# First routing's norms, turns and logits moved into the first attention's program

## The chip, the cores and the metric

The kernel runs on one core of a Trainium2 chip. The metric is device time in microseconds of one execution. In the rows PE is TensorE (PEld its weight loads), DVE is VectorE, ACT is ScalarE, POOL is GpSimd and SP is SyncE, which issues the transfers.

## The reference, cut to what matters

```python
x = x + attention0(layernorm(x), ctx, ctx, mask, Wq, Wk, Wv, Wo)       # 4 x 512 tokens of 256, 16 heads of 64
x = x + ffn0(layernorm(x), gate_w, gamma, beta, fc1s, b1s, fc2s, b2s)
x = x + attention1(layernorm(x), ...)
x = x + ffn1(layernorm(x), ...)

def ffn0(x, ...):                                   # 2048 tokens, 8 experts
    scores = (tanh(xf @ gate_w.T) + 1) * 0.5
    vals, idx = top_k(scores.T, 256)                # each expert picks its 256 tokens
    y = layernorm(xf[idx]) * gamma + beta           # then two layers, times vals, added to xf at idx
```

## The kernel before

Each layer is a program of its own (an `nc.Block`): all engines meet at its end. The first two matter here. All batches' x stay in SBUF as `T.x`, 16 tiles of 128 tokens by 256.

**`phase_attention0`** goes through 256 units in order. A unit `u` is 128 queries of one head against 512 keys; eight units (`UNITS`) make a head pair `g = u // 8`, `j = u % 8` counts within it, and eight pairs make a batch. Each engine has its instructions in an order written out by hand, and runs its loop over `u` with a lag: PE multiplies scores of u (`score`, L460), transposes the exponentials of u-3 (`turn`, L468) and multiplies them by the values of u-5 (`attend`). DVE takes the masked maximum of u (`maximum`, L677) and the low half of the transposed block of u-3 (L651), ACT the exponential of u (L576) and the high half of u-3 (L569). Most products are three fp16 products of high and low parts (`three_products`, L70 to L72). PE's score of u waits for the maximum of u-2 (two banks `sc`).

Between them stands side work, given by `side_work(g, j)` and done by PE at the end of unit (g, j): the k and q projections of the next pair at j = 0 and 1, a v projection for the next batch at j = 4, the output projection of the batch before at j = 5 (`w`, added to `T.x` by DVE), and the transposes of the next batch's normalized rows at j = 5 of pairs 5 and 6 (`z`). These groups use two banks `pj` in turn: a group waits until the one two places before it has been read (`open_group`). A `direct` group is read by ACT (high part) and DVE (low part) one unit later; the others go through ACT, POOL and SP. The statistics for the z groups are done on DVE in single steps (`late_statistics`): bn_stats, bn_aggr, and an inverse square root by an integer guess and three Newton steps, two steps in every three units from unit 6 of a batch on. After the last unit comes a tail: the last output projections (`late_products`), added to `T.x` by DVE (L778).

**`phase_route0`** then computes the layer norm of all four batches again (statistics L1067, L1070, Sqrt on ACT L944, norms on DVE L1085 and ACT L953), transposes it (L1009), copies it (L948), multiplies it in fp32 by the gate (`route`, L1016), takes Tanh (L974), and finds each expert's 256th largest score by a search of nine rounds: DVE compares all scores with seven candidates (`compare`, L1114), PE counts (L1031), DVE narrows (L1123 to L1127). After it come prefix sums on PE (L1034 to L1037), slots and lists of tokens (up to L1177). Beside the search ACT writes the expert rows `y` (L977) and the sum `T.x * (1 + rstd)` (L984), which SP stores (`acc`, `y`). SP's first loads, for this layer and the experts, stand at this program's start.

## Time and profile before

| what | us |
|---|---|
| three runs | 1173.72, 1176.66, 1181.28 (median 1176.66) |
| the profiled execution | 1175.02 |
| its span | 1173.1 |

By the page of the profile PE is busy for 91% of the span, DVE for 65%, ACT for 58%, POOL for 45%. The page cuts the span into 40 slices of 29.3 us. The first seventeen are the attention program; the granted clock, in tenths, is 9 in all of them and 8, 5 and 6 in slices 18 to 20, around the routing. A timeline row gives start and length in us; "x4" with one length is a run of instructions that follow each other, and the brackets name the engine's idle time just before and what ended it.

### The profile page before, as it was taken

Reading aid. Unit: us, or ns where it says so; the run is one execution under the profiler, and the core shown is the slowest. Engines: PE = TensorE matmul, PEld = TensorE weight load, DVE = VectorE, ACT = ScalarE, POOL = GpSimd, SP = SyncE. Lnnn points to the kernel's source line nnn. Section 1 sums busy time; section 2 is a strip of 40 time slices with the busy share of each in tenths; the row PEclk is TensorE's granted clock in tenths of the full one; section 3 lists DMA queues with packets and bytes.
Section 4 is the critical chain, followed back from the end, with each engine's and each line's share of the span. In section 5 each row is a group of like instructions: output and inputs, shape, how many; then the busy total and the mean of one; then the engine's idle time right before and its main releaser. Section 6 shows DMA issues by size and latency. Waiting matters only on the chain. (4 is left out here: it accounts for less than half of the span.)

```text
span 1173.1 us, 28682 instructions
## 1 busy us (share of the span) xinstructions
PE 1065.8 (91%) x10231; PEld 785.1 (67%) x10232; DVE 759.5 (65%) x2183; ACT 676.7 (58%) x1282; POOL 529.1 (45%) x599
## 2 busy tenths in 40 slices
PE   6999999999999999966699999698998866999996
PEld 3666777767777777666388886344454445888885
DVE  5888888888878877956611116668777774455553
ACT  6878876777768776837232216357667643343331
POOL 4677545465356433310147740566667523233312
PEclk9999999999999999985699999899999977999998
DMA  7633432333333422243546636624444241111110
GB/s 255 167 74 86 88 74 73 92 82 73 76 68 94 93 69 69 62 154 122 172 139 192 187 64 188 187 65 123 139 122 143 61 134 37 29 27 31 27 14 10
DMA packets 120027, 116.16 MB, mean 99 GB/s; under 512 B 43488, under 2 KB 100064, under 8 KB 119776
## 3 DMA queue, kind: packets, MB, share of 16 engines
q1 hardware_dynamic: 112608, 105.27, 31.9%
q0 software_dynamic: 7296, 9.25, 4.7%
q8 instruction: 77, 1.26, 0.4%
q14 instruction: 46, 0.38, 0.1%
HBM read 59.89 MB, written 21.82 MB: 70 GB/s over the span
## 5 line engine op out<-in xcount | busy, mean ns | idle before, releaser
L576 ACT ACTIVATE e<-masked,neg_max 128x512 f32<-128x512 f32 x256 | 184.4, 720 | 47.0 <-DVE neg_max L677 44.2
L651 DVE TENSOR_TENSOR e_t_lo<-et,e_t_hi 128x512 f16<-128x512 f32 x256 | 176.4, 689 | 46.1 <-ACT e_t_hi L569 43.9
L677 DVE CUSTOM_DVE_ANT_0 masked<-sc,mask_bias 128x512 f32<-128x512 f32 x256 | 175.3, 685 | 28.3 <-issue 24.5
L569 ACT ACTIVATE e_t_hi<-et 128x512 f16<-128x512 f32 x256 | 151.2, 591 | 68.3 <-PE et L468 67.0
L468 PEld LDWEIGHTS et<-ident,e 128*128 128x128 f32 x1024 | 124.5, 140 | 57.4 <-issue 8.9
L468 PE MATMUL et<-ident,e 128*128 128x128 f32 x1024 | 154.4, 273 | 1.2 <-ACT e L576 0.8
L2140 ACT ACTIVATE d_e<-d_st 128x384 f32<-128x384 f32 (+1 forms) x192 | 94.0, 526 | 49.4 <-PE d_st L2283 44.6
L70 PE MATMUL ob<-v_hi,e_t_hi 128*128 128x65 f16 x1024 | 119.0, 193 | 1.2 <-issue 1.2
L71 PE MATMUL ob<-v_lo,e_t_hi 128*128 128x65 f16 x1024 | 119.2, 193 | 0.0
L72 PE MATMUL ob<-v_hi,e_t_lo 128*128 128x65 f16 x1024 | 118.4, 193 | 0.0
L70 PE MATMUL h_hb<-h_xt_hi,experts_hi 128*128 128x256 f16 x352 | 96.8, 275 | 3.8 <-DVE h_xt_lo L2514 3.8
L460 PE MATMUL sc<-kk,qq 128*128 128x512 f16 x254 | 96.1, 378 | 2.9 <-DVE neg_max L677 1.9
L71 PE MATMUL h_hb<-h_xt_lo,experts_hi 128*128 128x256 f16 x352 | 96.8, 275 | 0.0
L72 PE MATMUL h_hb<-h_xt_hi,experts_lo 128*128 128x256 f16 x352 | 96.8, 275 | 0.0
L70 PEld LDWEIGHTS ob<-v_hi,e_t_hi 128*128 128x128 f16 x1024 | 95.7, 97 | 1.4 <-issue 1.4
L71 PEld LDWEIGHTS ob<-v_lo,e_t_hi 128*128 128x128 f16 x1024 | 94.5, 97 | 2.9
L461 PE MATMUL sc<-kk,qq 128*128 128x512 f16 x254 | 96.1, 378 | 0.0
L72 PEld LDWEIGHTS ob<-v_hi,e_t_lo 128*128 128x128 f16 x1024 | 94.7, 97 | 0.0
L2501 ACT ACTIVATE h_silu<-h_hb 128x256 f32<-128x256 f32 x88 | 33.7, 383 | 105.4 <-PE h_hb L72 105.4
L2288 PE MATMUL d_wk<-qk 128*128 128x384 f16 (+1 forms) x256 | 72.5, 311 | 12.5 <-PEq L1428 7.2
L2179 DVE TENSOR_REDUCE d_mx<-d_wk 128x1 f32<-128x384 f32 x128 | 66.3, 552 | 25.1 <-PE d_wk L2293 21.2
L2098 POOL TENSOR_SCALAR_AFFINE_SELECT d_e<-d_e 128x384 f32<-128x384 f32 x128 | 62.9, 521 | 43.0 <-ACT d_e L2140 42.9
(466 smaller groups left out, 2758.7 us busy)
## 6 DMA issues: line engine op xcount, KB each, us to landing
kk<-nat_k SPq DMA_DIRECT2D x64, 256.0 KB, 3.5
raw<-in_fc SPq DMA_DIRECT2D x16, 1024.0 KB, 7.5
qq<-nat_q SPq DMA_DIRECT2D x64, 128.0 KB, 2.4
qk<-scratch_stack SPq DMA_DIRECT2D x64, 128.0 KB
scratch_stack<-kq_hi SPq DMA_DIRECT2D x16, 256.0 KB, 3.0
scratch_stack<-kq_lo SPq DMA_DIRECT2D x16, 256.0 KB, 3.1
d_expert_raw<-in_gate_w SPq DMA_DIRECT2D x8, 512.0 KB, 3.8
d_expert_raw<-in_up_w SPq DMA_DIRECT2D x8, 512.0 KB, 3.9
```

Source lines behind the costliest of these rows:

```text
L70: pe.matmul(out, stat[0], mov[0], start=first, stop=False)
L71: pe.matmul(out, stat[0], mov[1], start=False, stop=False)
L72: return pe.matmul(out, stat[1], mov[0], start=False, stop=last)
L460: pe.matmul(sc[j % 2][:], stat, kk[g % 2][:, a, 0, :], start=True, stop=False)
L461: pe.matmul(sc[j % 2][:], stat, kk[g % 2][:, a, 1, :], start=False, stop=True).then_inc(scores, 1)
L468: mm = pe.transpose(et[u % 2][:, kt, :], e[u % NBUF][:, kt * P:(kt + 1) * P], T.ident[:])
L569: nc.scalar.activation(e_t[u % NBUF].hi[:], et[u % 2][:], ACT.Copy).then_inc(turned_hi, 1)
L576: nc.scalar.activation(e[u % NBUF][:], masked[u % NBUF][:], ACT.Exp, bias=neg_max[:, g % 2, j:j + 1], scale=-1.0).then_inc(exp_ok, 1)
L651: nc.vector.tensor_tensor(e_t[u % NBUF].lo[:], et[u % 2][:], e_t[u % NBUF].hi[:], ALU.subtract).then_inc(turned_lo, 1)
L677: nc.vector.tensor_tensor_reduce(masked[u % NBUF][:], sc[j % 2][:], mask_bias[g // PAIRS % 2][:, j % QT, :], -SCALE0, 3e38, ALU.add, ALU.m ...
L2140: nc.scalar.activation(part(e[n % EBUF][:, i // 3, :, :], i % 3), src, ACT.Exp, scale=SCALE1).then_inc(exp_ok, 1)
L2288: mm = pe.matmul(out[:, cols:cols + m * P], stat[n % QBUF][:, a, tile * P:(tile + 1) * P], mov[n % QBUF][:, a, start * P:(start + m) * P], ...
```

## The change

The first part of `phase_route0` goes into `phase_attention0`. Batches 0 to 2 become a new kind of side work, `r`: batch b's statistics are single steps on DVE once all its `w` groups are added, one step a unit from unit 40 of batches 1 and 2, two a unit from unit 40 of batch 3 (`late_steps`; 22 steps a batch, with one more variance than z). Their norms are ACT's, two units ahead of the group, and PE turns them at j = 7 of the first two pairs of the batch after next; for batch 2, at (30, 7) and (31, 3). The turned rows go to `T.z_t` as high and low fp16 parts. In the tail PE multiplies the logits of these 12 tiles as three fp16 products of 8 columns by the split gate; DVE puts the last batch's statistics between its last adds, the rest of the chain follows (Sqrt on ACT, reciprocal, norms on both, turns, parts, logits), and Tanh is the program's last step. `phase_route0` starts with the score. There ACT's `y` and `x` passes come first, with w_hi after the second batch; DVE's split of w1 moves behind the search and that of wo1 behind the first keys; POOL makes the first offsets first.

```diff
+LAST_ROUTE = [(PAIRS0 - 2, 7), (PAIRS0 - 1, 3)]
+LATE_AT, LATE_STEPS = 6, 2 * QT + 13
+ROUTE_AT, ROUTE_STEPS = 40, 2 * QT + 14
...
+    if j == 7 and b >= 2 and p < 2:
+        return "r", (b - 2, p)
+    if (g, j) in LAST_ROUTE:
+        return "r", (B - 2, LAST_ROUTE.index((g, j)))
     return None
+def late_steps(u):
+
+    b, at = u // (PAIRS * UNITS), u % (PAIRS * UNITS)
+    step, route = at - LATE_AT, at - ROUTE_AT
+    if b + 1 < B and step >= 0 and step % 3 < 2 and step // 3 * 2 + step % 3 < LATE_STEPS:
+        return [("z", b + 1, step // 3 * 2 + step % 3)]
+    if b >= 1 and route >= 0:
+        steps = (route,) if b + 1 < B else (2 * route, 2 * route + 1)
+        return [("r", b - 1, n) for n in steps if n < ROUTE_STEPS]
+    return []
...
+                sp.dma_start(gate_raw[:], dram["gate0"].rearrange("(c p) e -> p c e", p=P)).then_inc(gate_in, 16)
...
+                def turn_route(what):
+                    b, i = what[1]
...
+                    pe.wait_ge(r_act, 4 * b + 2 * (i + 1))
+                    for t in range(2):
+                        for c in range(DT):
+                            mm = pe.transpose(out[:, c * 2 * P + t * P:c * 2 * P + (t + 1) * P], late_z[b % 2][i][:, t, c * P:(c + 1) * P], T.ident[:])
+                    mm.then_inc(pj_full, 1)
...
+                def route(t):
+                    for c in range(DT):
+                        mm = three_products(pe, logit[:, t, :], (T.z_t.hi[:, c, t * P:(t + 1) * P], T.z_t.lo[:, c, t * P:(t + 1) * P]),
+                                            (gate_w.hi[:, c, :], gate_w.lo[:, c, :]), c == 0, c == DT - 1)
+                    return mm
...
+                        pe.wait_ge(direct_lo, len(DIRECT0))
...
                 pe.wait_ge(last_lo, 1)
                 for qt in range(QT):
                     late_products(qt, [CT - 1]).then_inc(late_full, 1)
+                pe.wait_ge(turned_lo, units)
+                pe.wait_ge(gate_lo, 1)
+                for t in range(NT - QT):
+                    route(t)
+                for i in range(2):
+                    if i == 0:
+                        pe.wait_ge(z_dve, 4)
+                    else:
+                        pe.wait_ge(r_act, 4 * (B - 1) + 2)
+                    for t in range(2):
+                        for c in range(DT):
+                            mm = pe.transpose(route_banks[i][:, c * 2 + t, :], early_z[2 * i + t][:, c * P:(c + 1) * P], T.ident[:])
+                    mm.then_inc(z_turned, 1)
+                for i in range(2):
+                    pe.wait_ge(z_lo, 2 + i + 1)
+                    for t in range(2):
+                        mm = route(NT - QT + 2 * i + t)
+                mm.then_inc(logits, 1)
...
-                    ahead = side_work(u // UNITS, u % UNITS + 2) if u < units and u % UNITS == 3 else None
+                    if u == GATE_AT:
+                        act.wait_ge(gate_in, 16)
+                        nc.scalar.activation(gate_w.hi[:], gate_raw[:], ACT.Copy).then_inc(gate_hi, 1)
+                    ahead = side_work((u + 2) // UNITS, (u + 2) % UNITS) if u + 2 < units else None
+                    if ahead is not None and ahead[0] == "r":
+                        b, i = ahead[1]
+                        act.wait_ge(late_ok, LATE0["r", b, ROUTE_STEPS - 1] + 1)
+                        act.wait_ge(pj_full, GROUP0["w", (b, QT - 1)] + 1)
+                        for t in range(2):
+                            route_norm(late_z[b % 2][i][:, t, :], b, 2 * i + t)
...
+                act.wait_ge(exp_ok, units)
+                nc.scalar.activation(warm, T.ident[:, 0:1], ACT.Sqrt)
                 act.wait_ge(last_turned, 1)
                 nc.scalar.activation(last_part.hi[:, CT - 1, :], last_bank[:], ACT.Copy).then_inc(last_hi, 1)
+                root(2, sd2)
+                act.wait_ge(shift_ok, 2)
+                for t in range(2, QT):
+                    route_norm(early_z[t], B - 1, t)
+                for i in range(2):
+                    act.wait_ge(z_turned, 2 + i + 1)
+                    cols = slice((B - 1) * S + i * 2 * P, (B - 1) * S + (i + 1) * 2 * P)
+                    nc.scalar.activation(T.z_t.hi[:, :, cols], route_banks[i].rearrange("p (c t) n -> p c (t n)", c=DT), ACT.Copy).then_inc(z_hi, 1)
+                nc.scalar.activation(warm, T.ident[:, 0:1], ACT.Tanh)
+                act.wait_ge(logits, 1)
+                nc.scalar.activation(T.route_tanh[:], logit, ACT.Tanh)
...
+                    done = LATE0[kind, b, n]
+                            dve.wait_ge(added, ADD0["w", (b, n)] + 1)
+                        y, roots, half, power = T.route_rstd[:, b, :, :].rearrange("p r t -> p (r t)"), sd2, halves2, square2
...
+                    elif kind == "r" and n == 2 * QT + 1:
+                        op = nc.vector.tensor_scalar(sd2[:, QT:2 * QT], mv[:, :, 1], 1.0 + EPS, EPS * EPS, ALU.mult, ALU.add)
...
-                        b, step = u // (PAIRS * UNITS) + 1, u % (PAIRS * UNITS) - LATE_AT
-                        if b < B and step >= 0 and step % 3 < 2 and step // 3 * 2 + step % 3 < LATE_STEPS:
-                            late_statistics(b, step // 3 * 2 + step % 3)
+                        if u == GATE_AT + 1:
+                            dve.wait_ge(gate_hi, 1)
+                            nc.vector.tensor_tensor(gate_w.lo[:], gate_raw[:], gate_w.hi[:], ALU.subtract).then_inc(gate_lo, 1)
+                        for step in late_steps(u):
+                            late_statistics(*step)
...
+                def last_statistics(qt):
+                    dve.wait_ge(added, len(ADD0) + qt + 1)
+                    nc.vector.bn_stats(stats[:, qt, :], T.x[:, (B - 1) * QT + qt, :]).then_inc(stat_ok, 1)
...
+                dve.wait_ge(late_ok, len(LATE0))
                 for qt in range(QT):
                     dve.wait_ge(late_full, qt + 1)
                     xt = T.x[:, (B - 1) * QT + qt, :]
                     nc.vector.tensor_tensor(xt, late[qt][:, 0:D], xt, ALU.add).then_inc(added, 1)
-
-
-EXPERTS0 = 8
+                    if qt >= 1:
+                        last_statistics(qt - 1)
+                last_statistics(QT - 1)
+                dve.wait_ge(stat_ok, 3 * QT)
+                for t in range(QT):
+                    nc.vector.bn_aggr(mv[:, t, :], stats[:, t, :]).then_inc(stat_ok, 1)
+                dve.wait_ge(stat_ok, 4 * QT)
+                nc.vector.tensor_scalar(sd, mv[:, :, 1], EPS, None, ALU.add).then_inc(stat_ok, 1)
+                nc.vector.tensor_scalar(sd2[:, QT:2 * QT], mv[:, :, 1], 1.0 + EPS, EPS * EPS, ALU.mult, ALU.add).then_inc(stat_ok, 1)
+                dve.wait_ge(stat_ok, 4 * QT + 2)
+                dve.sem_inc(var_ok, 1)
+                dve.wait_ge(sd_ok, 2)
+                nc.vector.reciprocal(T.route_rstd[:, B - 1, :, :].rearrange("p r t -> p (r t)"), sd2).then_inc(rstd_ok, 1)
+                dve.wait_ge(rstd_ok, 2)
+                route_shift(B - 1).then_inc(shift_ok, 1)
+                dve.wait_ge(exp_ok, units)
+                for t in range(2):
+                    nc.vector.tensor_scalar(early_z[t], T.x[:, (B - 1) * QT + t, :], mv[:, t, 0:1], T.route_rstd[:, B - 1, 0, t:t + 1], ALU.subtract, ALU.mult).then_inc(z_dve, 1)
+                for i in range(2):
+                    dve.wait_ge(z_hi, 2 + i + 1)
+                    cols = slice((B - 1) * S + i * 2 * P, (B - 1) * S + (i + 1) * 2 * P)
+                    nc.vector.tensor_tensor(T.z_t.lo[:, :, cols], route_banks[i].rearrange("p (c t) n -> p c (t n)", c=DT), T.z_t.hi[:, :, cols], ALU.subtract).then_inc(z_lo, 1)
...
-                sp.dma_start(gate[:], dram["gate0"].rearrange("(c p) e -> p c e", p=P)).then_inc(gate_in, 16)
...
+                def offset(r):
+                    pool.tensor_scalar(offsets[:, r, :], offs[:], float(CANDS + 1) ** -(r + 1), None, ALU.mult).then_inc(consts, 1)
+
                 pool.iota(offs[:], pattern=[[1, CANDS]], base=1, channel_multiplier=0, allow_small_or_imprecise_dtypes=True).then_inc(consts, 1)
-                pool.memset(zeros[:], 0.0)
+                pool.wait_ge(consts, 1)
+                offset(0)
+                pool.memset(ones[:], 1.0).then_inc(consts, 1)
+                for r in range(1, ROUNDS):
+                    offset(r)
+                pool.memset(zeros[:], 0.0).then_inc(consts, 1)
                 pool.memset(picks[:, NT, :], 0.0).then_inc(consts, 1)
...
-                nc.scalar.activation(warm[:, 0:1], T.ident[:, 0:1], ACT.Sqrt)
...
-                root(0)
...
-                for b in range(B):
-                    copy(2 * b)
-                    if b + 2 < B:
-                        root(b + 2)
-                    copy(2 * b + 1)
-                    if b + 2 < B:
-                        norm(b + 2)
-                    if b == 1:
-                        act.wait_ge(w_in, 16 * 3)
-                        nc.scalar.activation(T.w1.hi[:], raw[:, 0:2, :, :], ACT.Copy).then_inc(w_hi, 1)
-                        nc.scalar.activation(T.wo1.hi[:], raw[:, 2, :, :], ACT.Copy).then_inc(w_hi, 1)
-                    if b == B - 2:
-                        nc.scalar.activation(warm[:, 1:2], T.ident[:, 0:1], ACT.Tanh)
-                act.wait_ge(logits, 1)
-                nc.scalar.activation(score, logit, ACT.Tanh).then_inc(tanh_ok, 1)
...
                 for b in range(B):
                     for t in range(b * QT, (b + 1) * QT):
                         nc.scalar.activation(y[:, t, 0:D], T.x[:, t, :], ACT.Identity, bias=shift[:, b, 1, t % QT:t % QT + 1],
                                              scale=rstd[:, b, 1, t % QT:t % QT + 1]).then_inc(y_done, 1)
-                    act.wait_ge(more_ok, b + 1)
-                    act.wait_ge(xf_dve, 2 * (b + 1))
-                    act.wait_ge(xf_act, 2 * (b + 1))
+                    act.wait_ge(more_ok, 1)
                     act.wait_ge(y_done, (b + 1) * QT)
                     for t in range(b * QT, (b + 1) * QT):
                         op = nc.scalar.activation(T.x[:, t, :], T.x[:, t, :], ACT.Identity, bias=shift[:, b, 0, t % QT:t % QT + 1],
                                                   scale=more[:, b, t % QT:t % QT + 1])
                     op.then_inc(sum_done, 1)
+                    if b == 1:
+                        act.wait_ge(w_in, 16 * 3)
+                        nc.scalar.activation(T.w1.hi[:], raw[:, 0:2, :, :], ACT.Copy).then_inc(w_hi, 1)
+                        nc.scalar.activation(T.wo1.hi[:], raw[:, 2, :, :], ACT.Copy).then_inc(w_hi, 1)
...
-                def route(g):
-                    pe.wait_ge(copied, g + 1)
-                    for t in range(2 * g, 2 * g + 2):
-                        for c in range(DT):
-                            mm = pe.matmul(logit[:, t, :], xf_t[:, c, t * P:(t + 1) * P], gate[:, c, :], start=(c == 0), stop=(c == DT - 1))
-                    return mm
-
-                pe.wait_ge(gate_in, 16)
-                turn(0)
-                for g in range(NT // 2):
-                    if g + 1 < NT // 2:
-                        turn(g + 1)
-                    mm = route(g)
-                mm.then_inc(logits, 1)
-                pe.wait_ge(consts, TRI)
+                pe.wait_ge(consts, ONES)
...
+                pe.wait_ge(consts, TRI)
...
-                for b in range(B):
-                    nc.vector.tensor_scalar(more[:, b, :], rstd[:, b, 0, :], 1.0, None, ALU.add).then_inc(more_ok, 1)
-                dve.wait_ge(w_hi, 2)
-                nc.vector.tensor_tensor(T.w1.lo[:], raw[:, 0:2, :, :], T.w1.hi[:], ALU.subtract).then_inc(T.w1_split, 1)
-                nc.vector.tensor_tensor(T.wo1.lo[:], raw[:, 2, :, :], T.wo1.hi[:], ALU.subtract)
                 ahead(nc.vector.tensor_reduce(own[:], T.ident[:].rearrange("p (e d) -> p e d", d=DIGIT), AX.X, ALU.max))
-                ahead(nc.vector.tensor_reduce(eighth[:], T.ident[:].rearrange("p (j a) -> p a j", a=8), AX.X, ALU.max))
-                ahead(nc.vector.tensor_reduce(column[:], T.ident[:].rearrange("p (j a) -> p j a", a=8), AX.X, ALU.max))
-                dve.wait_ge(consts, OFFSETS)
+                nc.vector.tensor_scalar(score, T.route_tanh[:], 1.0, 0.5, ALU.add, ALU.mult).then_inc(score_ok, 1)
+                dve.wait_ge(consts, OFFSET0)
                 for h in range(2):
                     ahead(nc.vector.tensor_copy(cand[h][:], offsets[:, 0, :].unsqueeze(2).to_broadcast([P, CANDS, HE])))
                     ahead(nc.vector.memset(found[h][0][:, 0, :], 0.0))
                 dve.wait_ge(v, steps[0])
-                dve.wait_ge(tanh_ok, 1)
-                nc.vector.tensor_scalar(score, score, 1.0, 0.5, ALU.add, ALU.mult).then_inc(score_ok, 1)
                 dve.wait_ge(score_ok, 1)

...
                 compare(0)
                 compare(1)
+                nc.vector.tensor_scalar(more[:], rstd[:, :, 0, :], 1.0, None, ALU.add).then_inc(more_ok, 1)
+                    if r + 1 < ROUNDS:
+                        dve.wait_ge(consts, ONES + r + 1)
...
+                dve.wait_ge(w_hi, 2)
+                nc.vector.tensor_tensor(T.w1.lo[:], raw[:, 0:2, :, :], T.w1.hi[:], ALU.subtract).then_inc(T.w1_split, 1)
+                ahead(nc.vector.tensor_reduce(eighth[:], T.ident[:].rearrange("p (j a) -> p a j", a=8), AX.X, ALU.max))
+                ahead(nc.vector.tensor_reduce(column[:], T.ident[:].rearrange("p (j a) -> p j a", a=8), AX.X, ALU.max))
...
+                dve.wait_ge(consts, IDS)
...
+                nc.vector.tensor_tensor(T.wo1.lo[:], raw[:, 2, :, :], T.wo1.hi[:], ALU.subtract)
...
```

## Rows read from the trace of the kernel before

**Rows 1.** Stages: length, busy us (instructions) of each engine, clock, DMA share, GB/s
```profile
258.00:380.00 122.00, 121.98 (x1411) 90.05 (x1408) 99.42 (x316) 91.98 (x159) 63.65 (x69) 1.00 0.35 79
...
512.50:540.90 28.40, 20.24 (x96) 19.78 (x96) 15.09 (x71) 14.29 (x29) 3.28 (x16) 0.58 0.67 224
```
**Rows 2.** Timeline of DVE, from the last adds to the routing's end
```profile
510.96 0.75 DVE L778 TENSOR_TENSOR x<-sc,x 128x256 f32<-128x256 f32 x2 [0.60 <-PE sc L72]
...
512.70 1.40 DVE L1067 BATCH_NORM_STATS2 r_stats<-x 128x6 f32<-128x256 f32 x4 [0.32 <-PEq L233]
...
516.81 0.20 DVE L1080 RECIPROCAL r_rstd<-r_sd 128x8 f32<-128x8 f32 x1
...
530.28 1.22 DVE L1098 TENSOR_TENSOR w_lo<-r_raw,w_hi 128x1024 f16<-128x1024 f32 x1 [3.46 <-ACT wo_hi L970]
...
540.87 1.16 DVE L1114 TENSOR_TENSOR r_flags<-r_y,r_cand 128x448 f16<-128x448 f32 x2
...
566.10 0.17 DVE L1139 TENSOR_SCALAR r_need<-r_prefix_bank 128x8 f32<-128x8 f32 x1 [2.66 <-PE r_prefix_bank L1037]
...
576.90 0.17 DVE L1177 CAST slot_token<-r_slot_bank 128x16 int32<-128x16 f32 x1 [0.29 <-PE r_slot_bank L1048]
```
**Rows 3.** Timeline of ACT, the attention's tail and the routing's front
```profile
509.05 0.60 ACT L639 ACTIVATE o_t_hi<-pj 128x512 f16<-128x512 f32 x1 [5.81 <-PE pj L547]
512.67 1.28 ACT L940 ACT_TABLE_LOAD   x1 [3.03 <-PEq L233]
...
514.83 0.21 ACT L944 ACTIVATE r_sd<-r_sd 128x8 f32<-128x8 f32 x1 [0.66 <-DVE r_sd L1074]
517.25 1.09 ACT L953 ACTIVATE r_xf<-x,r_shift,r_rstd 128x256 f32<-128x256 f32 x2 [2.22 <-DVE r_shift L1083]
...
540.23 0.28 ACT L974 ACTIVATE r_y<-r_score_bank 128x128 f32<-128x128 f32 x1 [2.62 <-PE r_score_bank L1016]
```
**Rows 4.** Timeline of PE: transposes in the tail and in the front, search counts
```profile
508.35 0.65 PE L547 MATMUL pj<-ident,o 128*128 128x128 f32 x4 [0.73 <-DVE o L662]
...
523.62 1.09 PE L1009 MATMUL r_tb<-ident,r_xf 128*128 128x128 f32 x4
...
547.31 0.61 PE L1031 MATMUL r_count_bank<-r_flags,r_ones 128*128 128x28 f16 x16 [0.62 <-DVE r_flags L1114]
```
**Rows 5.** Stages again: head pairs 29 and 31, columns as in rows 1
```profile
459.78:473.05 13.27, 13.08 (x159) 9.21 (x157) 11.49 (x38) 10.66 (x20) 5.32 (x6) 1.00 0.30 70
...
486.16:497.53 11.37, 10.40 (x145) 7.70 (x144) 11.10 (x37) 9.58 (x17) 1.77 (x2) 1.00 0.12 24
```
**Rows 6.** DVE's groups, 30 to 380 us: short z steps; busy us, mean ns
```profile
L717 DVE TENSOR_TENSOR late_words<-n_rstd 128x4 f32<-128x4 f32 x9 | 5.2, 583 | 0.0
...
L721 DVE SCALAR_TENSOR_TENSOR n_rstd<-late_words,n_rstd 128x4 f32<-128x4 f32 x9 | 3.7, 416 | 0.0
...
L719 DVE SCALAR_TENSOR_TENSOR late_words<-late_words 128x4 f32<-128x4 f32 x9 | 2.6, 288 | 0.0
L711 DVE TENSOR_SCALAR late_words<-late_words 128x4 int32<-128x4 int32 x3 | 2.4, 807 | 0.0
```
**Rows 7.** One of these steps in the view of their tile: ns least/median/most
```profile
L719 DVE SCALAR_TENSOR_TENSOR late_words<-late_words x9: 145/152/948, 68.0 to 331.6; 128x4 f32<-128x4 f32 x9
```
**Rows 8.** Timelines of POOL and of DVE about 195 us
```profile
195.18 1.16 POOL L337 TENSOR_TENSOR nat_q<-raw,nat_q 128x512 f16<-128x512 f32 x1
...
195.55 0.80 DVE L717 TENSOR_TENSOR late_words<-n_rstd 128x4 f32<-128x4 f32 x1
```
**Rows 9.** Waits of PE (30 to 130 us), of DVE (138 to 499): total, times, longest
```profile
PE pj L70 <- DVE v_lo L732: 1.7, 2, 1.2
...
DVE z_t_lo L732 <- ACT z_t_hi L592: 2.5, 4, 0.7
```
**Rows 10.** Transfers from 512.5 to 578 us, and one stage among them
```profile
DMA packets 9031, 10.69 MB, mean 163 GB/s; under 512 B 1216, under 2 KB 8384, under 8 KB 8896
...
521.00:524.00 3.00, 2.11 (x10) 2.11 (x11) 2.79 (x14) 2.13 (x6) 0.00 (x0) 0.50 0.98 379
```

## What I expect, and why

> **What bounds the kernel now.** I read the table of stages first. In the attention program PE is busy for all of 122 us between 258 and 380, at clock 1.00, while DVE is busy for 99.4 and ACT for 92.0; the 120 us before and after look the same. So PE sets its pace. In the front of the routing (512.5 to 540.9) PE is busy for 20 of 28 us at clock 0.58, and no engine is the bound there [rows 1]. What is, the timelines show: a chain. The last adds end at 512.38, the statistics of all four batches start on DVE at 512.70, each batch goes through Sqrt, reciprocal and norms, PE transposes it and multiplies it in fp32 by the gate, ACT copies it between the two, and Tanh runs at 540.23; the first compare of the search starts at 540.87 [rows 2 to 4]. Last I asked what room the attention program has for the work that moves into it: a table by head pair [rows 5], the like steps that are there already [rows 6 to 8], and their waits [rows 9].
>
> **What the change takes away.** From the first of the four last adds (510.96) to the first compare (540.87) are 29.9 us [rows 2]. In the new order this stretch holds, on the path:
> - four adds and four statistics in turn on DVE, eight at 0.34 (two adds take 0.75, four statistics 1.40), the last one 0.41: 2.8;
> - aggregates and two tensor_scalars, from the statistics' end at 514.10 to ACT's Sqrt at 514.83: 0.7; Sqrt 0.25; reciprocal to ACT's first norm (516.81 to 517.25): 0.45 [rows 2, 3];
> - two norms on ACT 1.1 [rows 3]; four transposes of the second half, 0.65 at full clock (just after the attention) or 1.09 (in the front) [rows 4]. The logits of three batches now keep PE at work until shortly before them, so I take 0.7;
> - ACT's copy to the high part 0.6 [rows 3]; then DVE's low part (some 0.7, twice the 0.34 of an add, for twice its width) and 12 small products (at most 0.46, as 16 of the search's take 0.61 [rows 4]) beside the Tanh table load and its warm-up (1.28, as at 512.67, and 0.2, like a Sqrt). The table is the later: 1.5; Tanh 0.3 [rows 3];
> - the change of program 0.32 (DVE's idle time before 512.70); one reduction, the score and the first candidates, which DVE does in passes of 0.2 to 0.3: 0.8 [rows 2].
>
> Together 9.5, and 0.9 for hops between engines that I can't see: 10.4, bounds 9.9 to 11.4. **Gain 19.5 us (18.5 to 20.0).**
>
> Costed at nothing: the 72 small products for 12 tiles (72 x 0.038 = 2.7 us) on PE, which has nothing to do while DVE works out the last batch; uncovered they cost 2.7. The Sqrt table load (1.28) stands in ACT's 5.81 idle before 509.05 [rows 3]. The split of w1 (1.22) and two small reductions move to where DVE idles for 2.66 before 566.10 [rows 2]. The split of wo1, half as large, waits for nothing and would cost 0.6 uncovered. ACT's 32 row passes (16 x 1.09 us [rows 3]) start a little before the search as they did, and end before it. The gate's 8 KB and their split are two short passes in batch 0. SP's loads start some 8 us later, with the new routing program near 521 (the attention's growth left out), and what needs them is due 19 us earlier: 10.7 MB pass between 512.5 and 578, a busy stretch moves 379 GB/s [rows 10], so some 30 us from 522, over by 553, against the routing's new end near 557 (576.90 less 19.5).
>
> **What the change adds to the attention program**, where PE is the bound. Units count eight to a head pair, pairs 0 to 31.
> - *Six turns.* Four transposes take PE 0.65 [rows 4], some 0.5 of it alone since the next product overlaps the last; four of the turns lie where PE is bound: 2.0. A turn sits in unit 7, and the next pair's q product, two groups on, writes its bank, so PE waits for ACT's high and DVE's low part. The v groups of batch 0 sit in the same place and cost PE 1.7 us over four [rows 9]: 1.7 for four. ACT's two norms in a row delay its copies in pair 24: 0.3. Sum 4.0 (2.0, the transposes alone, to 6.0, every q product waiting 1.0).
> - *66 statistics steps on DVE*, 22 a batch. A statistic takes DVE 0.34, an aggregate 0.1, a short step about 0.1 with nothing in its way. But the like steps of the z batches run longer beside POOL: the one at 195.55 takes 0.80 and ends with POOL's subtraction, at 196.34 [rows 8]. The 27 Newton steps took 11.5 us, and at 0.152, the median of nine of them [rows 7], would have taken 4.1: 0.27 lost on each; the integer shift took 0.81 each time [rows 6]. I take 0.2 lost on a short step, as POOL is busy for only 5.3 of 13.3 us in pair 29 [rows 5].
>   - Batches 1 and 2, one step a unit from unit 40 of the batch: some 6 us a batch over three pairs, with DVE idle for 2.8 us a pair on average (22.6 over 122 us [rows 1]). PE needs a mask only two units later, so most of it fits: 0.3 a pair, 2.0 together (0.5 to 4.0).
>   - Batch 3, two steps a unit, in pairs 29 and 30. DVE's 1.8 idle us in pair 29 [rows 5] lie in units 0 and 1, where PE does the k and q products; in units 2 to 7 its instructions follow each other. What falls into units 0 and 1 (the four statistics, and in pair 30 four Newton steps) fits. The rest of pair 29 is 0.6 for four aggregates, 0.3, 0.95 with the integer shift, and 1.1 for four Newton steps: 2.8 after a little lead; of pair 30, 0.4, and 0.5 as ACT's norms come in between. Pair 31 has no projections, and DVE is busy for 11.10 of 11.37 us [rows 5]. Each of its two turns makes DVE wait for ACT's high part (0.7, the longest such wait [rows 9]) and then takes 0.6; the two norms (1.1) hold up ACT's copy of the turned block: 2.6 + 1.0. Sum 2.8 + 0.9 + 3.6 = 7.3 (5 to 10).
>
> A rule of the Trainium skill speaks against this change: SBUF — State Buffer, section Who interferes with whom, says that VectorE and GpSimd share one pair of ports under an exclusive lock, so that a VectorE instruction with two SBUF inputs, or in a two-port mode, blocks until the GpSimd instruction is through. The trace agrees: the short step ends with POOL's instruction [rows 8]. If each of 42 short steps met the start of a 1.16 us subtraction, they would add 49 us, not my 8.
>
> Sum of the additions 4.0 + 2.0 + 7.3 = **13.3 us** (7.5 to 20).
>
> **Result.** -19.5 + 13.3 = -6.2. The profiled execution took 1175.0 (span 1173.1 and 1.9 around it), so **1169 us**; the median of the runs shown is 1.7 above that execution, and they spread from 1173.7 to 1181.3. Corners: 1175.0 - 20.0 + 7.5 = 1162.5 and 1175.0 - 18.5 + 20.0 = 1176.5.
>
> **The rivals.**
> - *The side work is swallowed (faster).* DVE is idle for 1.8, 1.8 (pair 30 is like pair 29) and 0.3 us in the last three pairs, ACT for 2.6, 2.6 and 1.8 [rows 5], and the z steps left PE busy throughout [rows 1]. If only the turns' transposes and 2.5 us in pair 31 are seen, the growth is 4.5: 1175.0 - 19.5 + 4.5 = 1160. Against it: DVE's idle time is not where the two-a-unit steps lie.
> - *VectorE's short steps stall throughout (slower).* One mechanism: short steps that meet POOL's subtractions make DVE late, PE late behind it, and the next ones meet POOL again. At 1.0 us for each of 42 steps instead of 0.3 the growth is 13.3 + 29 = 42: 1175.0 - 19.5 + 42 = 1198. It makes the kernel 1% slower from 0.6 us of stall a step on, twice the 0.27 of [rows 6].
> - *The routing waits for its transfers.* With the front shorter, loads, sums and rows share 36 us. At the 224 GB/s of the old front as a whole [rows 1] the 10.7 MB need 48 us, end at 570, and 13 us of the gain go: 1182. Against it: the busy stretch moves 379 [rows 10].
>
> **How the numbers follow.** Some 1% (12 us) is what a measurement of this kernel can tell from no change. Forecast 0.63 (its own range 1162 to 1178, with the spread of runs), swallowed 0.23, stalls 0.09, transfers 0.05. Faster by over 1%: 0.23; within: 0.63 + 0.05 = 0.68; slower: 0.09. The range takes in the swallowed case and the forecast's upper corner with the spread of the runs: 1158 to 1180.
>
> **What would show it.** The first compare should start 10.4 us after the first last add; under 9.9 or over 11.4, and the front was mis-sized. That add should start near 524 instead of 511, 7 us of it from pairs 29 to 31, with DVE busy over 97% there; if those pairs grow by under 3, the swallowed case holds. PE's q products should wait for the new turns' low part. From compare to the last slot cast (540.87 to 576.90 [rows 2], 36.0 us) nothing should change; a wait for the row store at its end would show the transfers. I would be wrong most likely in DVE's stalls in the last batch.

## The result, and the profile after

The changed kernel takes 1169.29 us (median of five runs, 1166.24 to 1169.77) where the kernel before took 1176.66 beside it (1173.72 to 1181.28): a ratio of 0.9929, 95% interval 0.9911 to 0.9947. A second measurement gave 1168.02 (eight runs) beside 1174.99, a ratio of 0.9946 (0.9928 to 0.9965). Forecast were 1169 and "within 1%". That the median falls so near to 1169 is partly luck: the forecast was worked out for the profiled execution, 6.2 less than 1175.0, and that one came out 8.3 less.

The profiled execution took 1166.7 us, 8.3 less than the one before. Nearly all of that is decided by the first compare of the search, at 532.39 instead of 540.87 [rows 2]. The timeline of VectorE (start, duration, what; in brackets the idle time before it and what ended it) shows the end of the attention and the new front:

```profile
522.04 0.76 DVE L886 TENSOR_TENSOR x<-sc,x 128x256 f32<-128x256 f32 x2 [0.67 <-PE sc L75]
...
524.80 0.38 DVE L892 BATCH_NORM_AGGREGATE late_words<-late_words 128x2 f32<-128x6 f32 x4
...
525.78 0.20 DVE L899 RECIPROCAL route_rstd<-late_words 128x8 f32<-128x8 f32 x1 [0.33 <-ACT late_words L641]
...
528.67 0.69 DVE L908 TENSOR_TENSOR z_t_lo<-et,z_t_hi 128x512 f16<-128x512 f32 x1 [1.84 <-ACT z_t_hi L722]
...
531.47 0.29 DVE L1134 TENSOR_REDUCE r_own<-ident 128x8 f32<-128x128 f32 x1 [1.25 <-PEq L257]
...
532.39 1.16 DVE L1145 TENSOR_TENSOR r_flags<-r_y,r_cand 128x448 f16<-128x448 f32 x2
...
557.85 0.17 DVE L1177 TENSOR_SCALAR r_need<-r_prefix_bank 128x8 f32<-128x8 f32 x1 [1.10 <-PE r_prefix_bank L1106]
...
568.64 0.17 DVE L1218 CAST slot_token<-r_slot_bank 128x16 int32<-128x16 f32 x1 [0.29 <-PE r_slot_bank L1117]
```

Three lengths are read off here. From the first last add to the first compare: 532.39 - 522.04 = 10.35 us, where it was 29.91; forecast 10.4. From there to the last slot cast: 36.25, was 36.03; forecast no change. And the first last add itself stands at 522.04 instead of 510.96: the attention grew by 11.1 us; forecast 13.3. So 19.56 came off and 11.08 was paid.

Where the 11.1 us went can be seen finer than by pair, because TensorE transposes the exponentials of every unit and the starts of these transposes repeat from one execution to the next. I mark units by them ("29.1" is unit 1 of pair 29; they stand three units behind the mask and the side work that VectorE does meanwhile). The stretch between two marks, in us:

| stretch | what was put there | before | after | growth | forecast |
|---|---|---|---|---|---|
| start to 13.4 | gate split | 232.67 | 232.29 | -0.38 | 0 |
| 13.4 to 16.3 | 22 steps of batch 0 | 42.33 | 42.90 | 0.57 | 1.0 |
| 16.3 to 18.7 | two turns of batch 0 | 40.42 | 42.72 | 2.30 | 2.0 |
| 21.4 to 23.7 | 22 steps of batch 1 | 34.42 | 36.80 | 2.38 | 1.0 |
| 23.7 to 27.0 | two turns of batch 1 | 44.50 | 45.77 | 1.27 | 2.0 |
| 29 | 22 steps of batch 2 | 13.12 | 14.68 | 1.56 | 3.7 |
| 30.0 to 31.7 | two turns of batch 2 | 23.79 | 27.08 | 3.29 | 3.6 |
| 31.7 to first last add | | 8.96 | 9.03 | 0.07 | 0 |

(Between 18.7 and 21.4, and in pairs 27 and 28, nothing was added, and both kernels take 40.61 and 30.16. The stretch up to 13.4 took from 231.45 to 233.52 over all executions of this study, so its -0.38 says nothing.) Behind the last slot cast, where no code changed, this execution took 591.3 us up to GpSimd's last instruction and the one before 591.1; over all executions profiled for this study that same stretch took from 591.0 to 596.8. So a single whole time says little here to better than some 5 us. Stretches do.

The table of stages for pairs 29 to 31 (columns as in [rows 1, 5]) is the counterpart to before:

```profile
465.93:481.28 15.35, 14.15 (x160) 9.52 (x159) 14.77 (x54) 11.06 (x20) 5.30 (x6) 1.00 0.30 69
481.28:494.29 13.01, 12.73 (x158) 9.29 (x157) 12.03 (x44) 11.27 (x20) 5.31 (x6) 1.00 0.39 75
494.29:508.53 14.24, 11.46 (x149) 8.27 (x148) 12.48 (x39) 11.56 (x21) 1.77 (x2) 1.00 0.09 18
```

In pair 29 VectorE is now busy for 14.77 of 15.35 us and TensorE has 1.2 us idle: VectorE has become the bound. In pair 31 no engine is busy throughout (TensorE 11.46, VectorE 12.48, ScalarE 11.56 of 14.24): they wait for each other in turn.

### The profile page after: what moved, and what is told of

Read it like the earlier page. It is cut to its first block and busy times, and to the rows that moved or that the text cites. A ratio compares the mean times of both kernels' runs of the same rounds, so it can differ in the third digit from the quotient of the medians.

```text
span 1165.0 us, 28797 instructions
## 1 busy us (share of the span) xinstructions
PE 1055.8 (91%) x10263; PEld 770.9 (66%) x10264; DVE 771.1 (66%) x2213; ACT 679.0 (58%) x1286; POOL 530.4 (46%) x599
## 5 line engine op out<-in xcount | busy, mean ns | idle before, releaser
L2329 PE MATMUL d_wk<-qk 128*128 128x384 f16 (+1 forms) x256 | 72.6, 311 | 13.3 <-PEq L1469 8.0
```

The source lines that it names most:

```text
L2329: mm = pe.matmul(out[:, cols:cols + m * P], stat[n % QBUF][:, a, tile * P:(tile + 1) * P], mov[n % QBUF][:, a, start * P:(start + m) * P], ...
```

## The experiments

All kernels were profiled; e1 to e8 ran once each, so only their stretches are read, not their whole times. The stretches of the table above, for all of them (us; the last column is the first last add to the first compare):

| kernel | 13.4-16.3 | 16.3-18.7 | 21.4-23.7 | 23.7-27.0 | 27, 28 | 29 | 30-31.7 | front |
|---|---|---|---|---|---|---|---|---|
| before | 42.33 | 40.42 | 34.42 | 44.50 | 30.16 | 13.12 | 23.79 | 29.91 |
| after | 42.90 | 42.72 | 36.80 | 45.77 | 30.16 | 14.68 | 27.08 | 10.35 |
| after_again | 42.29 | 42.71 | 36.99 | 45.77 | 30.16 | 14.68 | 27.08 | 9.87 |
| e1 | 43.03 | 42.72 | 36.97 | 45.79 | 30.17 | 14.68 | 23.80 | 9.56 |
| e2 | 42.97 | 42.72 | 37.00 | 45.79 | 30.17 | 13.13 | 26.97 | 10.36 |
| e3 | 42.61 | 41.48 | 36.75 | 45.98 | 30.17 | 14.68 | 27.08 | 10.36 |
| e4 | 42.75 | 42.72 | 36.97 | 45.78 | 30.16 | 14.68 | 27.10 | 10.35 |
| e5 | 42.34 | 42.71 | 34.50 | 44.53 | 31.13 | 15.36 | 27.10 | 9.54 |
| e6 | 41.01 | 42.71 | 34.79 | 45.77 | 30.16 | 14.67 | 27.07 | 9.98 |
| e7 | 42.41 | 42.71 | 37.04 | 46.03 | 30.16 | 13.12 | 23.79 | 9.54 |
| e8 | 42.89 | 42.71 | 36.88 | 45.78 | 30.16 | 14.68 | 28.72 | 9.53 |
| e9 | 42.39 | 41.47 | 34.42 | 44.54 | 31.94 | 13.12 | 23.80 | 9.53 |
| e10 | 41.23 | 40.41 | 38.71 | 44.52 | 31.93 | 13.12 | 23.79 | 9.53 |
| e11 | 41.96 | 40.41 | 34.42 | 45.88 | 31.62 | 13.12 | 23.80 | 9.53 |

Where no edit touches a stretch it repeats to 0.03 us from 16.3 on, except 21.4 to 23.7 (36.75 to 37.04) and one case in e8, told below; 13.4 to 16.3 is looser, as masks land there at varying times.

**e1: batch 2's turns left out.**

```diff
-    if (g, j) in LAST_ROUTE:
-        return "r", (B - 2, LAST_ROUTE.index((g, j)))
...
```

> The changed kernel without the two turns of batch 2 in pairs 30 and 31 (its two turns, four norms, copies and low parts are left out, so the scores of batch 2 are made from other data). Reading the two traces unit by unit (theory A), the turns cost 3.3 us in pairs 30 and 31: the first last add, at 522.04 in the changed kernel, should start near 518.7. The prediction's own terms (theory B: 2.6 for the turned blocks and 1.0 for the norms) give nearly the same, 518.4. Rival (theory C): VectorE is late in pair 31 anyhow because of the steps before, and the turns only add their transposes, 2 x 0.65 = 1.3 us: 520.7.

Pairs 30 and 31 took 23.80 instead of 27.08: 3.28 less, and the same as before the change. The first last add stood at 520.32, not at 518.7: in this execution the pairs up to 16 ran 1.4 us longer. The transposes-only reading (1.3) falls. The price lies where the prediction put it, in the chain from ScalarE's copies to VectorE's low part. In the changed kernel, the timelines of ScalarE, VectorE and TensorE about the second turn:

```profile
498.23 1.08 ACT L647 ACTIVATE o_t_lo<-x,route_shift,route_rstd 128x256 f32<-128x256 f32 x2
499.21 0.57 ACT L630 ACTIVATE e_t_hi<-et 128x512 f16<-128x512 f32 x1
...
499.81 0.69 DVE L737 TENSOR_TENSOR e_t_lo<-et,e_t_hi 128x512 f16<-128x512 f32 x1 [0.48 <-ACT e_t_hi L630]
...
503.62 0.69 DVE L833 TENSOR_TENSOR z_t_lo<-pj,z_t_hi 128x512 f16<-128x512 f32 x1 [0.53 <-ACT z_t_hi L656]
...
504.99 0.39 PE L502 MATMUL sc<-kk,qq 128*128 128x512 f16 x1 [0.77 <-DVE neg_max L763]
```

The two norms (1.08) push ScalarE's next copy to 499.21, so VectorE waits 0.48; later it waits 0.53 for the copy of the turned block and spends 0.69 on its low part; 0.77 of that reach TensorE as a wait for the next mask. By unit each turn costs 1.12, its norms 0.53 to 0.57.

**e2: batch 2's steps left out.**

```diff
-    if b >= 1 and route >= 0:
+    if b >= 1 and b + 1 < B and route >= 0:
...
```

> The changed kernel without the 22 statistics steps of batch 2, two a unit in pairs 29 and 30 (left out; the norms of its turns use the figures of batch 1, so the scores of batch 2 are other ones). Theory A, unit by unit: the steps cost 1.6 us, all of it in units 1 to 4 of pair 29, and the first last add moves from 522.04 to 520.5. Theory B, the prediction: 2.8 in pair 29 and 0.9 in pair 30, 3.7 us: 518.3. Rival (theory C): the delay of pair 29 is what makes the turns of pairs 30 and 31 dear, so more than 3 us go, and the turns get cheaper than 1.6 us each.

Pair 29 took 13.13 (1.55 less, all in units 1 to 4), pairs 30 and 31 only 0.11 less. So the steps cost 1.66 and not the 3.7 forecast, and the turns cost the same without the steps ahead of them: the two prices are separate. What the prediction had too high is seen in the timeline of VectorE in pairs 29 and 30 of the changed kernel:

```profile
477.47 0.16 DVE L806 TENSOR_SCALAR late_words<-late_words 128x8 int32<-128x8 int32 x1
477.66 0.59 DVE L808 TENSOR_SCALAR route_rstd<-late_words 128x8 int32<-128x8 int32 x1
...
479.39 0.15 DVE L814 TENSOR_TENSOR late_words<-route_rstd 128x8 f32<-128x8 f32 x1
479.57 0.17 DVE L816 SCALAR_TENSOR_TENSOR late_words<-late_words 128x8 f32<-128x8 f32 x1
```

Of the 14 short steps one, the guess, ran longer than 0.17; the integer shift took 0.16 where it had taken 0.81 in the z batches [rows 6].

**e3: batch 0's and 1's turns one unit earlier.**

```diff
-    if j == 7 and b >= 2 and p < 2:
+    if j == 6 and b >= 2 and p < 2:
```

> The changed kernel with the four turns of batches 0 and 1 in unit 6 instead of unit 7 of their pairs (nothing left out). Theory A: TensorE's q product, which follows two groups later in the same bank, now finds the low part done; the two waits seen there (1.04 us in pair 16, 0.37 in pair 24) go and the pairs 16 to 18 and 24 to 26 get 1.4 us shorter; the transposes themselves (4 x 0.47 to 0.65) stay. Theory B, the prediction's term: 1.7 us. Rival (theory C): the norms now stand beside the copies of the w groups of unit 5 and hold ScalarE up there, so that the wait only moves, and less than 0.4 us goes.

In the waits of TensorE between 204 and 510 us of the changed kernel (what, on what, total, times, longest) the forecast wait is there:

```profile
PE pj L73 <- DVE z_t_lo L833: 1.1, 2, 0.9
```

One unit earlier it is gone, and batch 0's turns cost 1.06 instead of 2.30. Batch 1's, however, cost 1.48 instead of 1.27. In pair 24 the norms stand right before one of ScalarE's copies of a turned block (ScalarE's timeline of e3):

```profile
398.52 1.08 ACT L647 ACTIVATE o_t_hi<-x,route_shift,route_rstd 128x256 f32<-128x256 f32 x2
399.50 0.57 ACT L630 ACTIVATE e_t_hi<-et 128x512 f16<-128x512 f32 x1
```

VectorE waits 1.03 for that copy, and unit 24.3 got longer by 0.98. So the outcome of theory A came in pair 16 and that of theory C in pair 24, though not by copies of w groups, which pair 24 doesn't hold. Together 1.03 were won, less than the 1.4 and 1.7 forecast.

**e4: the narrow gate products done twice. e8: ten wide products in their place.**

```diff
                 for t in range(NT - QT):
                     route(t)
+                for t in range(NT - QT):
+                    route(t)
```

```diff
                     if i == 0:
+                        pe.wait_ge(normed, 2 * PAIRS0)
+                        for _ in range(10):
+                            pe.matmul(ob[1][:].rearrange("p t n -> p (t n)"), T.wk0.hi[:, 0, 0:P], T.ctx_t.hi[:, 0, 0:512], start=True, stop=True)
```

> The changed kernel with the 72 gate products of the first twelve tiles done twice in the tail (the second time with the same result), so that TensorE has work while VectorE and ScalarE make the last batch's norms (in the changed kernel it idles for 2.18 us there). Theory A: the granted clock stays at 1.00 from 524 to 531 where it fell to 0.50, the two groups of transposes take 0.65 us instead of 1.11 and 1.06, and the first compare comes 0.5 to 0.9 us sooner: 9.5 to 9.9 us after the first last add instead of 10.35. Rival (theory C): the load of the Tanh table (1.28 us) on ScalarE ends last in any case, or the clock falls nonetheless, and 10.2 to 10.4 us stay.

> The changed kernel with ten products of 128 x 512 elements whose result nobody reads, on TensorE between the gate products of the first twelve tiles and the last batch's transposes (nothing left out). Repeating the narrow gate products there left the granted clock at 0.50 from 526 on. Theory A: products of the attention's own width keep it at 1.00 as they did until 524; the two groups of transposes take 0.65 us instead of 1.11 and 1.06, and first compare comes 9.6 to 10.0 us after the first last add instead of 10.35. Rival (theory C): the clock falls to 0.50 near 526 whatever TensorE does in these two microseconds, since it is the thin work before them that counts: 10.3 to 10.6.

With the narrow products (one execution) TensorE's idle time before the transposes fell from 2.18 to 0.35 us, but the granted clock fell all the same and the front took 10.35. With the wide ones it took 9.53. In the table of stages (columns as above, the clock is the third number from the end), first the changed kernel, then e8:

```profile
524.00:526.00 2.00, 0.71 (x29) 0.61 (x25) 1.58 (x10) 0.21 (x1) 0.00 (x0) 1.00 0.00 0
526.00:528.00 2.00, 1.11 (x5) 1.11 (x6) 0.81 (x3) 1.09 (x2) 0.00 (x0) 0.50 0.00 0
```

```profile
526.00:528.00 2.00, 2.00 (x33) 1.18 (x30) 1.56 (x11) 0.21 (x1) 0.00 (x0) 1.00 0.00 0
528.00:530.00 2.00, 1.95 (x12) 1.03 (x10) 0.77 (x3) 1.58 (x3) 0.00 (x0) 1.00 0.00 0
```

But 9.53 and 9.54 were also reached without the wide products, by e5 and e7; e5 has the changed kernel's own tail. There the two groups of transposes took, in the timeline of TensorE,

```profile
524.60 0.66 PE L613 MATMUL et<-ident,masked 128*128 128x128 f32 x4 [2.19 <-DVE masked L908]
525.10 0.64 PE L613 MATMUL pj<-ident,masked 128*128 128x128 f32 x4
```

against 1.11 and 1.06 in the changed kernel's. So the front's length goes by when the clock falls after the attention. By the windows of one microsecond it fell 3.9 to 4.5 us after the first last add in after, e2, e3 and e4, 5.3 in e6, 5.5 in after_again, 5.8 to 6.3 in e1, e5 and e7; the front took 10.35 or 10.36 in the first four, 9.98 in e6, 9.87 in after_again, and 9.56 to 9.54 in the last three. In the four kernels with wide products (e8 to e11) it fell 8.5 to 11.2 us after that add, and all four took 9.53. That the products hold the clock up is thus supported by four executions of four; what they are worth is 0 to 0.8 us, by the execution.

**e5: batch 1's steps and turns later.**

```diff
-    if j == 7 and b >= 2 and p < 2:
-        return "r", (b - 2, p)
+    if j == 7 and b == 2 and p < 2:
+        return "r", (0, p)
+    if j == 7 and b == 3 and 3 <= p < 5:
+        return "r", (1, p - 3)
...
+    if b + 1 == B and 0 <= step < ROUTE_STEPS:
+        return [("r", 1, step)]
...
```

> The changed kernel with the 22 steps of batch 1 moved from the last units of the third batch (pairs 21 to 23) to units 6 to 27 of the fourth (pairs 24 to 27), where VectorE is busy for about 80% and no z step stands, and its two turns to unit 7 of pairs 27 and 28 (nothing left out). Theory A (a step costs only where VectorE has no room): the 2.37 us that pairs 21 to 23 had grown by go, and pairs 24 to 28 grow by no more than 0.4 for the steps; the turns cost 0.47 each, as in pair 25, instead of 0.80 and 0.47: together 2.3 to 2.7 us less up to pair 29. Theory B, the prediction's 2.0 us for both batches: 1.0 less. Rival (theory C): short steps that meet GpSimd's work hold VectorE up wherever they stand, and less than 0.8 us goes.

Pairs 21 to 23 gave back 2.30, and 23.7 to 27.0, which now hold the 22 steps instead of the two turns, took 44.53, 0.03 more than before the change with neither. So the same steps cost 2.3 us in one place and nothing in another, though some of them ran long here too (0.61 for the guess, 0.81 for the last step, the norms' shift, 0.53 on average over the three of one Newton line). The turns cost 0.97 in pairs 27 and 28. Then pair 29 grew by 0.68, as the last turn's low part meets batch 2's statistics there. Up to pair 29 that is 2.6 less than in the changed kernel, as theory A has it, and 1.9 with pair 29.

**e6: short steps of batches 0 and 1 replaced by aggregates.**

```diff
+                    elif kind == "r" and b < 2:
+                        op = nc.vector.bn_aggr(square2[:, 0:2], stats[:, n % QT, :])
...
```

> The changed kernel with the 14 short steps of batches 0 and 1 (shifts and Newton steps) replaced by as many small aggregates, which in the changed kernel took 0.16 to 0.18 us 24 times out of 24 and never met GpSimd; their figures are constants, so the scores of these two batches are other ones. Rivals on what the steps of pairs 21 to 23 cost (2.37 us): theory A, half of it and more is the time in which a short step stands beside GpSimd's work (seven of batch 1's fourteen took 0.65 to 0.90 instead of 0.16, 4.1 us more): without that 0.6 to 1.1 us of growth is left there. Theory C: it is the number of steps in a stretch where VectorE has no room, and 1.9 us or more is left.

Growth left in 21.4 to 23.7: 34.79 - 34.42 = 0.37 of 2.38. The stretch 13.4 to 16.3 took 41.01, where the ten executions with the steps there took 42.29 to 43.03. So most of the price is the time a short step stands beside GpSimd. The cause is visible in the changed kernel; first GpSimd's timeline, then VectorE's:

```profile
250.76 1.12 POOL L362 TENSOR_TENSOR v_lo<-raw,v_hi 128x512 f16<-128x512 f32 x1
...
252.51 1.16 POOL L370 TENSOR_TENSOR o_parts<-o,o_parts 128x512 f16<-128x512 f32 x1
```

```profile
250.95 0.94 DVE L814 TENSOR_TENSOR late_words<-route_rstd 128x8 f32<-128x8 f32 x1
...
253.04 0.65 DVE L816 SCALAR_TENSOR_TENSOR late_words<-late_words 128x8 f32<-128x8 f32 x1
```

The steps end at 251.89 and 253.69, GpSimd's subtractions at 251.88 and 253.67. Among the 28 short steps of the two batches twelve took 0.65 to 0.94 instead of 0.16, 7.2 us more in all, and each of the twelve ended within 0.03 us of the end of one of GpSimd's subtractions. The aggregates in their place took, in the list of VectorE's groups (busy, mean ns),

```profile
L800 DVE BATCH_NORM_AGGREGATE late_words<-late_words 128x2 f32<-128x6 f32 x28 | 4.8, 171 | 0.0
```

The rule that the prediction weighed (the Trainium skill, SBUF — State Buffer, section Who interferes with whom) also says that a VectorE instruction with at most one SBUF input, outside the two-port modes, does not contend with GpSimd. The trace agrees: 171 ns on average for all 28, in the units where the short steps had been held up; 18 of the 28 began while GpSimd was at an instruction.

**e7: batch 2 in the tail.** Its statistics and aggregates stand one at a time behind the adds that they need (pairs 25 to 29). The rest follows the attention's last unit, with ScalarE's square root instead of the Newton steps, banks that are free by then, and the second low part in the gap ahead of the last batch's:

```diff
+LAST_STEPS = {15: 0, 16: 4, 23: 1, 24: 5, 31: 2, 32: 6, 39: 3, 40: 7}
...
+                root(2, sd2)
+                act.wait_ge(shift_ok, 2)
...
+                for t in range(QT):
+                    route_norm(late_z[0][t // 2][:, t % 2, :], B - 2, t)
                 act.wait_ge(last_turned, 1)
...
+                last_low(1)
                 for i in range(2):
                     dve.wait_ge(z_hi, 2 + i + 1)
...
```

> The changed kernel with batch 2 out of the attention's last three pairs: its four statistics and four aggregates stand one at a time in pairs 25 to 29 behind the adds that they need, and the rest (root on ScalarE with the last batch's table instead of the Newton steps, norms, turns, low parts) in the tail, where VectorE idles for 1.5 and 3.7 us, ScalarE for 4.3 and TensorE for 0.7 (nothing left out). Theory A: pairs 29 to 31 give back 1.6 + 3.3 = 4.9 us, the tail from the last unit's low part to the first last add (7.77 us from 514.27 to 522.04) grows by at most 0.2, and from there to the first compare 0.2 to 0.8 us come on top of 10.35 (one low part of 0.69 and some copies near the last batch's): 4.0 to 4.6 us earlier at the first compare. Rival (theory C): the tail is a chain without room, the four norms, two turns, two copies and two low parts (some 2.1, 1.3, 1.2 and 1.4 us) lengthen it by over 3 us, and less than 2 us is left of the gain.

Pairs 29 to 31 took exactly what they took before the change (13.12, 23.79), the statistics cost 0.26 in 23.7 to 27.0, the tail from the last unit's low part to the first last add 7.76 us (7.77 in the changed kernel), and the front 9.54. The timelines of ScalarE and of VectorE show where the work went:

```profile
510.73 0.19 ACT L655 ACTIVATE late_words<-late_words 128x8 f32<-128x8 f32 x1
511.39 1.09 ACT L661 ACTIVATE o_t_hi<-x,route_shift,route_rstd 128x256 f32<-128x256 f32 x2 [0.47 <-DVE route_shift L846]
512.39 1.08 ACT L661 ACTIVATE o_t_lo<-x,route_shift,route_rstd 128x256 f32<-128x256 f32 x2
```

```profile
516.36 0.68 DVE L912 TENSOR_TENSOR z_t_lo<-et,z_t_hi 128x512 f16<-128x512 f32 x1
...
521.82 0.68 DVE L912 TENSOR_TENSOR z_t_lo<-ob,z_t_hi 128x512 f16<-128x512 f32 x1
...
526.65 1.16 DVE L1185 TENSOR_TENSOR r_flags<-r_y,r_cand 128x448 f16<-128x448 f32 x2
```

The norms fill ScalarE's wait of 4.3 us; the low parts fill 0.67 us ahead of the first last add and part of the 1.84 ahead of the last batch's. The chain-without-room rival falls. The expected 0.2 to 0.8 us of growth in the front didn't come either; that the front was 0.8 shorter goes with the clock's late fall (6.3 us after the add), as in e1 and e5.

**e9: the moves together. e10: batch 0's steps moved too. after_again: the changed kernel beside them.** In e10 the steps of batch 0 stand, two at a time, in every third unit of pairs 17 to 20:

```diff
...
+    if b == 2 and step >= 0 and step % 3 == 2:
+        return [("r", 0, n) for n in (step // 3 * 2, step // 3 * 2 + 1) if n < ROUTE_STEPS]
...
```

> What the single runs gave, together (nothing left out): batch 0's turns in unit 6 of pairs 16 and 17 (1.2 us less there), batch 1's steps and turns in pairs 24 to 28 (2.3 less), batch 2 in the tail (4.9 less in pairs 29 to 31), and eight products of 128 x 512 between the gate products and the last transposes, into a bank that is free by then, which keep the clock up (0.8 less against the profiled execution of the changed kernel, where it fell early). Theory A (the costs stand in separate places and add): 9.2 us less, first compare near 523, time near 1159 to 1161 where the changed kernel had 1169.3, a ratio to the kernel before of 0.985 to 0.987. Rival (theory C): the gains were one execution's luck or take each other's room (batch 1's steps and batch 2's statistics share pairs 27 to 29), and less than 5 us is left.

> The same as the run with all moves, and batch 0's 22 steps also moved: from pairs 13 to 15, where they cost 1.7 us, to the units of pairs 17 to 20 that hold no z step, two a unit, with words of their own, and its turns to unit 7 of pairs 21 and 22 (nothing left out). Theory A: VectorE has some 3 us of room in each of these pairs, so the 1.7 us go and at most 0.3 comes back: 1.4 us less than the run with all moves. Rival (theory C): two steps in one unit, beside z steps in the two others, hold VectorE up as in pair 29 (0.3 us and more a unit, eleven units), and it is 1 to 2 us slower than that run.

> The changed kernel itself beside the two (nothing changed or left out), for its spread from execution to execution. Its front was 10.35 us with the clock falling 3 us after the first last add; in another run whose tail is the same code the clock fell 6.6 us after it and the front took 9.53. Theory A: the front takes between 9.5 and 10.4 us, by when the clock falls, and the pairs 16 to 31 repeat to within 0.1 us a unit. Rival (theory C): the front's length has another cause, and with the clock falling early it is shorter than 10, or the costs by unit don't repeat.

e9: 1160.44 us (1157.67 to 1161.03), ratio to before 0.9872 (0.9848 to 0.9897), where the changed kernel had 0.9946 (0.9928 to 0.9965) on the same chip. The gains add, except that batch 1's turns and batch 2's statistics, now neighbours, cost 1.78 in pairs 27 and 28 instead of 0.97. e10: 1161.81, 0.9891 (0.9867 to 0.9914). Its steps cost nothing: 16.3 to 18.7 took 40.41, as before the change, and 13.4 to 16.3 gave 1.2 back against e9 (e11, with the same steps moved, only 0.4). But its turns, in pairs that hold a z turn, cost 4.29 together, where they had cost 1.05 in e9. So neither reading of e10 was right: it was the turns, not the pairs of steps, that made it no better. The waits of TensorE from 204 to 505 us in e10:

```profile
PE pj L74 <- DVE z_t_lo L871: 2.6, 3, 1.1
```

after_again repeated the changed kernel's stretches to 0.03 us from 16.3 on, but for 21.4 to 23.7 (0.19 more), and its front took 9.87 with the clock falling 5.5 us after the add (read in finer windows than in the expectation, the two falls named there stood at 4.0 and 6.2).

**e11: e10 with its four turns alone, one in each of pairs 25 to 28.**

```diff
+    if j == 7 and b == 3 and 1 <= p < 5:
+        return "r", ((p - 1) // 2, (p - 1) % 2)
...
```

> The run with batch 0's steps moved too, mended where its profile showed new costs (nothing left out): there the steps cost nothing in pairs 17 to 20 (no unit of pairs 16 to 20 got longer), but its two turns cost 2.1 us each in pairs 21 and 22, which hold a z turn already (the first 0.63 + 0.22 + 1.25, by unit); and batch 2's statistics beside batch 1's turns cost 0.58 and 0.23 in pairs 27 and 28. Here all four turns stand alone, one in unit 7 of each of pairs 25 to 28, and batch 2's statistics stand in units without a turn's low part. Theory A (a turn alone costs its transposes, 0.47, and DVE's steps cost nothing where it has room): 2 x 1.6 + 0.8 = 4 us less than that run, first compare near 520.6, time near 1158. Rival (theory C): a turn in each of four pairs following each other, beside the w groups and batch 1's steps, is dear again, and less than 1.5 us is gained.

1159.10 us (1158.39 to 1161.57), ratio 0.9862 (0.9838 to 0.9887): better than the changed kernel, and not to be told from e9. From pair 16 on the side work now costs 2.9 us over the kernel before (1.38 in 23.7 to 27.0, 1.46 in pairs 27 and 28, 0.07 at the end), where the changed kernel paid 10.9. Against e10 3.2 us went (4.29 in pairs 21 and 22, less 1.36 for two turns in pairs 25 and 26, and 0.31 in pairs 27 and 28), not 4: q products still wait a little behind these turns,

```profile
PE pj L74 <- DVE z_t_lo L867: 0.5, 2, 0.3
```

and unit 6 of pairs 26 and 28 is 0.38 and 0.52 longer than before. The first compare stood at 523.49 and not at 520.6, as this execution ran 2.2 us longer than e10's up to 16.3, before the moved turns.

## Why the prediction was right, step by step

*The front: right in sum, one term by luck.* ScalarE's and TensorE's timelines of the changed kernel give the terms:

```profile
525.54 0.21 ACT L641 ACTIVATE late_words<-late_words 128x8 f32<-128x8 f32 x1 [4.89 <-DVEq L897]
526.22 1.09 ACT L647 ACTIVATE masked<-x,route_shift,route_rstd 128x256 f32<-128x256 f32 x2 [0.47 <-DVE route_shift L823]
528.04 0.60 ACT L722 ACTIVATE z_t_hi<-et 128x512 f16<-128x512 f32 x1 [0.73 <-PE et L609]
528.89 0.60 ACT L722 ACTIVATE z_t_hi<-pj 128x512 f16<-128x512 f32 x1 [0.26 <-PE pj L609]
529.51 1.28 ACT L723 ACT_TABLE_LOAD   x1
...
530.91 0.26 ACT L725 ACTIVATE route_tanh<-et 128x128 f32<-128x128 f32 x1
```

```profile
526.89 1.11 PE L609 MATMUL et<-ident,masked 128*128 128x128 f32 x4 [2.18 <-DVE masked L904]
527.79 1.06 PE L609 MATMUL pj<-ident,masked 128*128 128x128 f32 x4
```

Adds and statistics took 2.72 (forecast 2.8), from there to Sqrt 0.78 (0.7), to the first norm 0.68 (0.70), the change of program 0.30 (0.32), from it to the compare 0.92 (0.8). The table and Tanh followed in 1.68 (1.8). Only from the first norm to the end of the copies was it 3.27 where norms, transposes and copy made 2.4. In e5, which has the same tail and whose clock fell later, ScalarE's timeline shows 2.45 for it (523.93 to 526.38):

```profile
523.93 1.09 ACT L651 ACTIVATE masked<-x,route_shift,route_rstd 128x256 f32<-128x256 f32 x2 [0.47 <-DVE route_shift L827]
525.30 0.60 ACT L726 ACTIVATE z_t_hi<-et 128x512 f16<-128x512 f32 x1 [0.27 <-PE et L613]
525.79 0.59 ACT L726 ACTIVATE z_t_hi<-pj 128x512 f16<-128x512 f32 x1
```

So 0.82 of the 0.87 goes with the clock: I took 0.7 for the transposes, as at full clock, and here they ran at half of it. TensorE had idled for 2.2 us ahead of them in both executions. The copy of the other half, which I had left out, adds next to nothing with the clock up. The 0.9 "for hops that I can't see" happened to be that 0.87. With the clock up the front takes 9.53, which is the 9.5 of the sum without these 0.9, and below my lower bound of 9.9; the bounds should have been set by the two clocks. The gate products of twelve tiles, at no cost in the sum, started from 522.75 to 524.54, while TensorE had nothing else; the split of w1 (1.22 us) fits where VectorE still waits 1.10 afterwards. No wait for the row store, the loads or the sums appears: the transfer rival (1182) falls.

*The turns of batches 0 and 1: right (4.0 forecast, 3.57 measured),* and by its own parts: transposes 0.47 each where 0.5 was said, the q products' waits 1.04 and 0.37 where 1.7 was said, 0.32 by the norms (0.3 said, but in pair 24; it came in pair 16).

*The steps of batches 0 and 1: the step that failed.* Forecast 2.0; their price is about 3.4. Of it e5 gave back 2.30 for batch 1's. For batch 0's, ten executions with the steps in 13.4 to 16.3 took 42.29 to 43.03 there, 42.66 on average, and e10 and e11, without them, 41.23 and 41.96: about 1.1, not to be told better than from 0.3 to 1.8. Only 2.95 of growth shows, as TensorE in the kernel before had waited 1.03 in pair 14 for VectorE, behind GpSimd, which had got a mask late. The loss on a short step was sized well, 0.26 on average against 0.2 and 0.27; over all 42 short steps, batch 2's included, it was 7.7 us, where the prediction had 8, and 49 if every step met a subtraction. What was wrong is the 0.3 a pair behind "most of it fits": I set 6 us a batch against VectorE's idle time averaged over a batch, 2.8 us a pair. The last pairs of a batch have less: in the kernel before VectorE is busy for 11.34 of 12.87 us in pair 23, and in the changed kernel for 13.08 of 13.20:

```profile
373.63:386.50 12.87, 12.86 (x159) 9.42 (x158) 11.34 (x37) 11.24 (x21) 8.78 (x11) 1.00 0.36 83
```

```profile
378.17:391.37 13.20, 12.80 (x155) 8.76 (x153) 13.08 (x43) 10.62 (x19) 7.61 (x11) 1.00 0.36 82
```

*Batch 2's steps: mis-sized the other way.* 3.7 forecast, 1.6 measured. I gave every short step the mean loss of the z batches and the integer shift its 0.81; in pairs 29 and 30 one of 14 ran long, and behind the last of them (29.5 to 29.7) nothing grew. A mean loss doesn't belong to a step: it is whether this step starts during one of GpSimd's subtractions or casts.

*Batch 2's turns: right (3.6 forecast, 3.3 measured),* mechanism and size, as e1 shows. The check that went with them, VectorE busy for over 97% in pairs 29 to 31, was wrong: it was 96, 92 and 88%. In pair 31 the chain goes through all three engines.

So 13.3 became 11.1 with errors against each other: the steps of batches 0 and 1 grew the kernel by 0.95 more than forecast (their price is 1.4 above it; the wait of before and the scatter of 13.4 to 16.3 take back the rest), batch 2's by 2.1 less, the turns by 0.7 less, and the start was 0.4 shorter. The swallowed case (pairs 29 to 31 growing by under 3) falls: they grew by 4.9. Stalls throughout fall as a runaway, 0.26 us a step and not 0.6; as a local price they make up most of what the steps of batches 0 and 1 cost.

## What to carry to other kernels

Price side work at the units where it stands, not by an engine's mean idle time: the same 22 small steps cost 2.3 us in pairs 21 to 23 and nothing in pairs 24 to 27, and a turn cost 0.47 us alone and 2.1 beside another. Before work is put into a loop that has no room, look at the waits of its tail: batch 2's steps, norms, turns and low parts cost 4.9 us in the last three pairs; with its statistics and aggregates spread over pairs 25 to 29 and the rest in the tail they cost 0.26. And where whole times scatter by 0.5%, marks that repeat (here the transposes of each unit) tell gains of a tenth of a microsecond apart.

## What was not expected of the hardware

- The granted clock fell 4.0 to 6.2 us after the first last add in executions whose tail is all but the same code (after, after_again, e1, e2, e3, e5, e6), and the front varied with it from 10.36 to 9.54 us.
- Once it fell within the attention: in e8 (one of the fourteen executions), whose last pairs are the changed kernel's own, the clock was 0.50 from 508 us on and 0.69 on average from 510 to 512, and the unit that takes 2.79 us in the changed kernel took 4.43. TensorE had been busy for 1.15 and 1.22 of 2.00 us in the two stretches before, as in the changed kernel, where the clock stayed at 1.00.

```profile
506.00:508.00 2.00, 1.22 (x18) 1.11 (x19) 2.00 (x7) 1.43 (x3) 1.48 (x2) 0.96 0.00 0
508.00:510.00 2.00, 2.00 (x20) 1.75 (x19) 1.42 (x4) 1.44 (x3) 0.28 (x1) 0.50 0.53 108
510.00:512.00 2.00, 2.00 (x15) 1.55 (x14) 0.18 (x1) 0.00 (x0) 0.00 (x0) 0.69 0.12 23
```

- The small aggregates never ran long: 0.17 to 0.18 us, 24 times out of 24 in the changed kernel and 28 out of 28 in the places of e6's short steps, where arithmetic on eight words took up to 0.94.
